# Embedding lookups in gathers of 64 rows instead of 128, in a DLRM tower on one Trainium2 core

## The reference

```python
e = jnp.stack([tbl_0[ids[:, 0]], tbl_1[ids[:, 1]], ..., tbl_31[ids[:, 31]]], axis=1)   # (512, 32, 64)
for i, (W, b) in enumerate(zip(Ws, bs)):
    nxt = jnp.einsum('bjk,bzk,ojz->bok', h, inp, Wr) + b[None, :, None]
    if i != n_layers - 1:
        h, o = (nxt[:, :O // 2], nxt[:, O // 2:])
    else:
        o = nxt
    outs.append(o)
z = jnp.sum(jnp.concatenate(outs, axis=1), axis=2)
h = jnp.concatenate([z, dense_ctx], axis=1)
h = jnp.maximum(h @ W_top1 + b_top1, 0.0)
h = jnp.maximum(h @ W_top2 + b_top2, 0.0)
y = h @ W_top3
```

## Time and profile before

| | us |
|---|---|
| median of 3 runs (675.22 to 676.35) | 675.24 |
| the profiled execution, its own time | 675.91 |
| its span in the trace | 674.2 |
| PE busy | 636.4 |
| DVE busy | 482.4 |
| ACT busy | 215.0 |
| POOL busy | 129.6 |

### The profile page before, as it was taken

The page is one execution under the profiler, slowest core; times in us unless marked ns, Lnnn a source line. Parts: engine busy times, 40 slices in busy tenths (PEclk is TensorE's granted clock), DMA queues, the critical chain, the costliest instruction groups (busy, mean ns, idle before and its releaser), DMA issues.

```text
span 674.2 us, 36102 instructions
## 1 busy us (share of the span) xinstructions
PE 636.4 (94%) x16536; PEld 508.0 (75%) x16536; DVE 482.4 (72%) x490; ACT 215.0 (32%) x351; POOL 129.6 (19%) x137
## 2 busy tenths in 40 slices
PE   5834899999999999999999999999999999999998
PEld 5833668787788888787878787878887878888873
DVE  4237878787888888887888888888888888862000
ACT  2330333344333333433333333333333233333012
POOL 7755034444443543200000000000000000000000
PEclk9686999999999999999999999999999999999999
DMA  5110010001000110000000000000000000002000
GB/s 179 28 27 18 11 26 19 20 21 27 21 21 18 26 23 21 18 11 9 9 8 8 8 8 8 8 8 8 5 6 5 7 8 8 8 8 72 11 2 0
DMA packets 13228, 12.74 MB, mean 19 GB/s; under 512 B 5745, under 2 KB 10465, under 8 KB 12946
## 3 DMA queue, kind: packets, MB, share of 16 engines
q1 hardware_dynamic: 9010, 8.09, 4.6%
q0 software_dynamic: 4192, 4.25, 2.8%
HBM read 8.03 MB, written 0.00 MB: 12 GB/s over the span
## 4 chain that ended last, share of the span: by engine, by line
PE 90%; POOL 5%; issue 3%; DVE 2%; DMA 1%; ACT 0%; DVEq 0%; POOLq 0%
PE psX L325 20%; PE psT L384 19%; PE psT L368 8%; PE psT L408 8%; PE psT L394 7%; PE psT L371 5%; POOL G_sb L229 5%; PE psX L368 5%; PE psX L337 4%; PE psX L371 4%; PE psX L458 2%; PE psX L347 1%; PE psX L263 1%; PE psX L487 1%; DVE PT L709 1%
## 5 line engine op out<-in xcount | busy, mean ns | idle before, releaser
L388 PE MATMUL psT<-T_sb,W1d 64*64 64x256 f32 x1024 | 233.4, 378 | 0.0
L384 PE MATMUL psT<-T_sb,W1d 64*64 64x256 f32 x1024 | 233.4, 378 | 0.0
L394 PE MATMUL psT<-T_sb,W1d 64*64 64x256 f32 (+3 forms) x2048 | 204.4, 299 | 0.0
L673 DVE TENSOR_TENSOR prod<-X 128x1024 f32 (+4 forms) x202 | 170.7, 914 | 18.2 <-PE psT L371 18.1
L709 DVE STREAM_TRANSPOSE PT<-prod 128x4608 f32<-128x4608 f32 x32 | 159.0, 4969 | 0.0
L384 PEld LDWEIGHTS psT<-T_sb,W1d 64*64 64x64 f32 x1024 | 131.4, 133 | 26.3 <-issue 14.1
L325 PE MATMUL psX<-PT,W0T 32*64 32x256 f32 x4608 | 135.5, 382 | 10.1 <-DVE PT L709 9.1
L408 PE MATMUL psT<-T_sb,W1d 64*64 64x64 f32 (+2 forms) x1536 | 141.7, 270 | 0.0
L325 PEld LDWEIGHTS psX<-PT,W0T 32*64 32x64 f32 x4608 | 111.8, 133 | 36.0 <-issue 26.5
L388 PEld LDWEIGHTS psT<-T_sb,W1d 64*64 64x64 f32 x1024 | 131.4, 133 | 0.0
L394 PEld LDWEIGHTS psT<-T_sb,W1d 64*64 64x64 f32 x2048 | 123.7, 133 | 0.8
(11 more groups left out here) (79 smaller groups left out, 569.8 us busy)
## 6 DMA issues: line engine op xcount, KB each, us to landing
X<-T_sb SPq DMA_DIRECT2D x64, 64.0 KB, 1.9
G_sb<-in_L_rec_W SPq DMA_DIRECT2D x2, 1024.0 KB, 6.6
E_q<-in_tbl,ids_g POOLq DMA_INDIRECT x96
prod<-in_W_top SPq DMA_DIRECT2D x2, 512.0 KB, 3.7
G_sb<-in_L_rec_W SPq DMA_DIRECT2D x1, 512.0 KB, 5.8
G_sb<-in_tbl,ids POOLq DMA_INDIRECT x32, 2.4
dT<-dT SPq DMA_DIRECT2D x3, 32.0 KB
zb<-in_L_rec_b SPq DMA_DIRECT2D x4, 0.2 KB
```

The lines of the kernel that those rows point to most:

```text
L384: mm(psT[low, 0, 0:HF * SMP], W1d[low, HF + k, :], cross.rearrange("p v (z y) s -> p v z y s", y=HF)[:, :, :, k, :], start=start, stop=sto ...
L388: mm(psT[high, 0, 0:HF * SMP], W1d[low, k, :], T_flat[low, SMP * row:SMP * (row + HF)], start=start, stop=stop, tile_position=(0, C))
L394: last = mm(out[:, SMP * 4 * a:], W1d[high, HF * v + k, :], T_flat[high, SMP * (row + 4 * a):SMP * (row + HF)], start=start, stop=stop and ...
L673: return tt(out, x[:, :, z0:z0 + nz].unsqueeze(3).broadcast_to(shape), x[:, :, y0:y0 + ny].unsqueeze(2).broadcast_to(shape), ALU.mult)
```

## The change

The gathers of groups 1 to 3 are cut in two: for each field one gather for the samples on partitions 0 to 63 and one for those on 64 to 127. As both take their indices from partitions 0 to 63, `ids_g` becomes 64 partitions by two columns of 32 indices, filled by one DMA with a rearranged source. PE's wait counts twice as many gathers. Group 0 is as it was.

```diff
-        ids_g = sb("ids_g", [P, NF], INT32)
+        ids_g = sb("ids_g", [C, 2, NF], INT32)
...
-                    pool.dma_start(ids_g[:, :], ids[bass.ds(g * P, P), :]).then_inc(idsg_in, 16)
+                    pool.dma_start(ids_g[:, :, :], ids[bass.ds(g * P, P), :].rearrange("(h p) z -> p h z", h=2))\
+                        .then_inc(idsg_in, 16)
...
                 for z in range(FQ * q, FQ * q + FQ):
-                    nc.gpsimd.indirect_dma_start(
-                        out=E_q[:, z - FQ * q, :], out_offset=None, in_=tables[z],
-                        in_offset=bass.IndirectOffsetOnAxis(ap=ids_g[:, z:z + 1], axis=0),
-                    ).then_inc(rows_in, 16)
+                    for h in range(2):
+                        nc.gpsimd.indirect_dma_start(
+                            out=E_q[C * h:C * h + C, z - FQ * q, :], out_offset=None, in_=tables[z],
+                            in_offset=bass.IndirectOffsetOnAxis(ap=ids_g[0:C, h, z:z + 1], axis=0),
+                        ).then_inc(rows_in, 16)
...
-                    pe.wait_ge(rows_in, 16 * FQ * (n + 1))
+                    pe.wait_ge(rows_in, 2 * 16 * FQ * (n + 1))
```

## The result

The changed kernel takes 736.5 us (median, 734.5 to 738.7) against 675.4 us: a ratio of 1.090, 95% interval 1.088 to 1.092, 61 us slower. The profiled executions differ by 735.1 - 674.2 = 60.9 us of span.

What follows compares the result with a forecast made beforehand. PE was taken to bound lookup passes at 18.0 us; after the change, eleven rings (237.2 us) plus long gathers (4.5) replace 200.0 us: +41.7 on the 675.24 us median, 717 us, range 688 to 740.

Steps and rivals of the forecast that it cites:

- ring of one E_q: Lookup pass: PE transposes, POOL gathers into E_q, rows land; 12.6 us before against PE's 18.0, forecast 21.1 after.
- the first lookup: Group 1, quarter 0: rows land near 70.3 us, 73 with slow gathers; PE asks at 81.80, so no cost.
- a fixed 1 us: POOL's idle time before a quarter, from transposes to gather, was to fall to this from 9 us.
- the all-fixed rival: Gather time does not scale with rows, 0.95 us (0.93 and up): +58.4 us, 734 us, at worst 741; chance 0.22.
- the middle of 0.76 and 0.95: 64-row gather taken as 0.855 us, between only the index part halving (0.76) and nothing scaling with rows (0.95).
- long gathers: Gathers above the 947 ns median, clustered near each group's sixth; taken to add 4.5 us in the lookup passes.
- by instruction: Slow-gather clusters follow the instruction count: five of six lie in the lookup passes after the change, 6.4 us.
- by rows: Slow-gather clusters follow the row count: two of three lie in the lookup passes, 2.6 us.
- clock: PE's lower clock lengthens the transposes by 0.45 us, at most 11 times, 5 us; taken as zero.
- my forecast's band: 64-row gather of 0.78 to 0.93 us, +27 to +57 us, so 702 to 732 us; chance 0.50.
- The landing of rows and the number of transfers: Sign of error in kind: E_q rows land much later than 1.4 us after the last gather, transfers being doubled.
- The hidden cases: Lookups stay under PE's pass: proportional gathers (0.475 us), 675 to 677 us, chance 0.08; or faster, at most 673.5, chance 0.02.

## Why the prediction was right, and where its size was off

**The mechanism.** Right in the main: PE had no wait on rows, the ring of one E_q had 5.4 us to spare, 16 gathers overdraw it, and the cost is paid eleven times and not in the first lookup. PE, after and before, has the same work. Two things it had wrong or lacked: that DVE's products lengthen gathers, and POOL's idle time before a quarter, which I put at a fixed 1 us. It is 2.8 to 3.4 us, because it takes in the landing as well as the hand-over, 1.42 + 1.47 = 2.9 us in my own ring. The run with half the gathers shows that the new form alone is free, the one with half the fields split shows that added gathers cost little until the spare time is used up.

**The size.** I forecast 717 us, 41.7 us more; the kernel became 61 us slower. The range to 740 held the measured 736.5, but only because I had drawn it wide enough for the all-fixed rival, whose reason (d = 0.95) did not come true: that is luck, not a forecast. The sum in its own terms, against 58.5 us measured between first and last transposes:

- as predicted: 41.7
- d, the duration of a 64-row gather: 0.902 us instead of 0.855. 16 x 0.047 x 11 = 8.3 us more. This was the step "I take the middle of 0.76 and 0.95": I granted that half of the 0.38 us by which a gather exceeds a plain DMA goes with the rows. The rows take 1 ns each; the index part is nearly all constant. The row count halves a term of 0.13 us, not of 0.38 or 0.95.
- long gathers: 192 x (0.957 - 0.902) = 10.6 us, of which 9.9 lie in the rings, where I had 4.5: 5.4 us more. I scaled a cluster "by instruction" or "by rows". It is neither: they come with DVE's products, and the change brings them about. Before, a quarter's gathers were over 9.7 us after they began, ahead of the products in a regular pass; now they last 20 us and reach into the products of each of the eleven passes.
- clock: seven of the eleven rings begin with transposes of 1.04 to 1.12 instead of 0.66 us, 3.1 us, which I had named and set at zero.

That is 41.7 + 8.3 + 5.4 + 3.1 = 58.5, the measured change of the stretch. (Two small errors cancel in it: the gaps between gathers sum to 0.7 us more than I had, the landings to 0.5 less.) The rest of the 60.9 is 2.0 us in the stretch after it, where the clock is low once more behind PE's last wait (0.94 over its first 28 us), and 0.4 us ahead of it, which I can't tell from scatter.

**The rivals.** The duration lies inside my forecast's band (0.78 to 0.93), the time does not (702 to 732): it lies near the 734 us of the all-fixed case, which got there with d = 0.95 and fewer long gathers. The landing of rows and the number of transfers are out by the steady 1.33 to 1.45 us of landing and by the run with two buffers, PE's clock by the waits of 2.1 to 6.6 us in which its slower work is hidden, all but the 3.1 us above and the 2.0 us after the last ring. The Trainium skill ("DMA: Bandwidth & Descriptors", "Anatomy of one DMA") calls descriptor generation small and variable; the run with four sizes agrees as far as rows go, with 1 ns a row beside 0.83 us that no row count changes. The hidden cases needed d under 0.66 and are out. The rule against halves of the partitions (the Trainium skill, "DMA: Bandwidth & Descriptors", "Rules for kernel authors") holds here too, though for another reason than the one it gives, the DMA engines that both halves share: what binds here is POOL's issuing.

## What to carry to other kernels

Where gathers are issued from GpSimd, count instructions, not rows: here 1.13 us for each and 1 ns for each row. A stage with one buffer is a ring; add its issue, its landing and its hand-over before calling added work hidden, and do not expect a price in proportion: here the first half of the added gathers cost 12 us and the second half 49. When a stage grows longer, ask what it now runs beside: most gathers were not slow in the old trace because they ended before DVE's products began.

## What the runs showed of the hardware

A gather that POOL issues beside a DVE product with both factors in SBUF is held up: mostly 1.16 to 1.7 instead of 0.90 us beside products of 0.9 us each, and 2.86 instead of 0.95 beside one of 2.29 us. Beside the long one the gather ends 0.81 to 0.83 us after the product in eight traces of eight, so it seems to do most of its work only when the product is over. With one factor in PSUM, the same product holds nothing up (0.94 and 0.95 us in two kernels). The Trainium skill ("SBUF — State Buffer", "Who interferes with whom") says that a DVE instruction with two SBUF inputs contends with a GpSimd instruction that reads SBUF; the indices of a gather lie there, and the traces agree; that it is the reading of these indices that waits is argued, not shown. Copies of DVE from SBUF to SBUF held some gathers (1.10 to 1.30 us) and not others; what decides that I did not try. After waits of PE of 2.1 to 6.6 us the transposes behind them ran at the lower of the two clock levels (1.11 us) or not (0.66 us, behind waits of 2.09, 3.40, 3.47 and 3.50 us), so the wait's length alone does not tell.
